# Eight edits to a state-space and two-expert kernel: spare rows, biases, register checks, a skewed addition and a spread tail

## The reference

```python
probs = softmax(layernorm(x) @ Wg)              # 8 experts
top_vals, top_idx = top_k(probs, 2)             # renormalised to sum 1: the shares
h = relu(layernorm(x) @ W1[e] + b1[e])          # 128 -> 256
y = h @ W2[e] + b2[e]                           # 256 -> 128
out = x + layernorm(share_a * y_a + share_b * y_b)
```

## Time and profile before

| | us |
|---|---|
| median of three runs | 990.61 |
| profiled execution | 989.48 |
| its span | 987.6 |
| PE busy | 836.5 (85%) |
| DVE busy | 769.7 (78%) |
| ACT busy | 659.0 (67%) |
| POOL busy | 521.9 (53%) |

### The profile page before, as it was taken

The page is one execution under the profiler, slowest core; times in us unless marked ns, Lnnn a source line. Parts: engine busy times, 40 slices in busy tenths (PEclk is TensorE's granted clock), DMA queues, the critical chain, the costliest instruction groups (busy, mean ns, idle before and its releaser), DMA issues.

```text
span 987.6 us, 26130 instructions
## 1 busy us (share of the span) xinstructions
PE 836.5 (85%) x8010; PEld 693.0 (70%) x8010; DVE 769.7 (78%) x2323; ACT 659.0 (67%) x1592; POOL 521.9 (53%) x1031
## 2 busy tenths in 40 slices
PE   4699999999999999999999999755787998989870
PEld 2487887777777777777777777544677888878770
DVE  5577879899998998989989899847667566656660
ACT  4578888777787787777877778533435556556650
POOL 4344544455454554646455555433456666666664
PEclk9799999999999999999999999986779999999995
DMA  7000000001010120210000000050624555555520
GB/s 204 8 2 4 5 2 15 7 29 44 8 54 15 55 77 9 86 23 10 10 12 8 12 7 9 19 144 18 171 64 123 153 137 141 141 141 142 146 87 0
DMA packets 59298, 57.82 MB, mean 59 GB/s; under 512 B 16727, under 2 KB 42861, under 8 KB 59163
## 3 DMA queue, kind: packets, MB, share of 16 engines
q1 hardware_dynamic: 54203, 47.61, 18.3%
q0 software_dynamic: 4960, 8.54, 2.5%
HBM read 44.52 MB, written 19.91 MB: 65 GB/s over the span
## 4 chain that ended last, share of the span: by engine, by line
DVE 30%; PE 21%; issue 20%; POOL 16%; SPq 6%; DMA 3%; ACT 2%; POOLq 1%; DVEq 0%; ACTq 0%
POOL out_dram L2249 8%; PE bank L875 4%; DVE xt L785 4%; DVE mg L1047 4%; POOL moe_y L2246 4%; DVE ob L1126 3%; PE bank L672 2%; SPq L1714 2%; DMA rows<-csplit 2%; DVE y L1059 2%; DVE state L1074 2%; PE bank L859 2%; DVE ob L1100 2%; PE bank L674 2%; PE bank L673 1%
## 5 line engine op out<-in xcount | busy, mean ns | idle before, releaser
L1038 POOL TENSOR_TENSOR y<-y,zt 128x256 f32<-128x256 f32 x64 | 46.7, 729 | 225.7 <-issue 136.4
L2249 POOL DMA_INDIRECT out_dram<-moe_y,moe_token x91 | 92.2, 1013 | 74.1 <-POOL moe_y L2246 69.4
L672 PE MATMUL bank<-thi,whi 128*128 128x512 f32 x224 | 105.7, 472 | 15.8 <-DVE cs L809 8.0
L2156 PE MATMUL bank<-moe_w,moe_hid 128*128 x728 | 117.3, 298 | 0.1
L959 ACT ACTIVATE m<-bank 128x512 f32<-128x512 f32 x128 | 69.3, 592 | 70.7 <-PE bank L861 70.5
L2117 PE MATMUL bank<-moe_h_turned,moe_w_now 128*128 128x128 f32 x728 | 103.8, 288 | 12.6 <-DMA moe_w_now<-pair_weights 12.5
L2117 PEld LDWEIGHTS bank<-moe_h_turned,moe_w_now 128*128 128x128 f32 x728 | 93.9, 202 | 16.4 <-issue 14.4
L2156 PEld LDWEIGHTS bank<-moe_w,moe_hid 128*128 128x128 f32 x728 | 98.2, 196 | 4.9 <-issue 0.4
L1047 DVE TENSOR_TENSOR mg<-bank,m 128x512 f32<-128x512 f32 x128 | 82.3, 685 | 17.5 <-PE bank L875 16.5
L674 PE MATMUL bank<-thi,wlo 128*128 128x512 f32 x224 | 89.7, 401 | 0.0
L673 PE MATMUL bank<-tlo,whi 128*128 128x512 f32 x224 | 89.6, 400 | 0.0
(11 more groups left out here) (268 smaller groups left out, 2361.0 us busy)
## 6 DMA issues: line engine op xcount, KB each, us to landing
moe_w_now<-pair_weights SPq DMA_DIRECT2D x91, 258.0 KB, 2.9
moe_block_in<-pair_rows SPq DMA_DIRECT2D x91, 66.0 KB, 1.9
pair_weights<-in_L_ffn_W_dram SPq DMA_DIRECT2D x31, 128.0 KB
parts<-csplit SPq DMA_DIRECT2D x128, 4.0 KB
rows<-csplit SPq DMA_DIRECT2D x128, 4.0 KB
pair_rows<-spare_row SPq DMA_DIRECT2D x29, 66.0 KB
out_dram<-moe_y,moe_token POOLq DMA_INDIRECT x91, 2.6
pair_rows<-xall,row_index POOLq DMA_INDIRECT x64, 2.6
```

The lines of the kernel that those rows point to most:

```text
L672: PE.matmul(bank[:], whi[:, w], thi[:], start=True, stop=False)
L2156: mm = PE.matmul(o, hid[:, u % HID, k, n, :], w2[:, bass.ds(e, 1), n, :].rearrange("p o d -> p (o d)"), start=False, stop=n == FB - 1, ski ...
L2249: PL.indirect_dma_start(rows_out, bass.IndirectOffsetOnAxis(token[:, u % IN:u % IN + 1], 0), y[:, u % YR, :], None, bounds_check=TOK - 1, ...
```

## The change

Eight edits. (1) The 29 writes of spare rows move from the end of the first half into `sp_pair_weights`, one group after its last part (n = NE + 1). (2) `b2` is no longer loaded as a broadcast, split and multiplied; it is stored beside `b1` in `pair_weights` (three bias columns for each expert), so that it comes with the unit's weights, and the product with `thirds` becomes a matmul in transpose mode of the broadcast bias column with the identity. `act_prepare` and `dve_prepare` are gone, and a weight slot is free again only when `pe_down` of unit u - 6 is done. (3) The register loads of SyncE and TensorE carry no runtime bounds check. (4) `pool_out` is cut in two: GpSimd adds unit u and then issues the DMA of unit u - 1 (`pool_return`). (5) The inputs of the shares are worked out before the scatter, three more operations in `pool_gap` for each group and one more column in each row; `pool_shares` becomes `pool_tokens`, which makes the row numbers alone, and `act_shares` reads the rows' columns. (6) IN is 24. (7) Units 0 to 19 have their relu on ScalarE, odd ones too. (8) The steps of the tail are spread further apart on every engine, and `pe_skip` and the second table move with them. The first residual stays on VectorE. Of the tail's steps the diff below shows TensorE's; on VectorE the top-two steps of the last two groups move from 3 and 4 to 4 and 5, and from 7 and 8 to 9 and 10, the last group's statistics from 5 to 6, and the row indices from 6 and 10 to 8 and 13 (the second table to 13 and 14). On GpSimd the last three groups' scatters move from 1, 6 and 10 to 3, 8 and 13. On ScalarE each logits step moves one to two later.

```diff
-ROW = D + 4
-WROW = 2 * FH + 2 * FB
-C_TOK, C_GAP, C_BIAS, C_SCALE = D, D + 1, D + 2, D + 3
+ROW = D + 5
+PCOLS = FB + 1
+WROW = 2 * FH + 2 * PCOLS
+C_TOK, C_BIAS, C_SCALE, C_UPPER, C_LOWER = D, D + 1, D + 2, D + 3, D + 4
...
+            sp.dma_start(b_rank[:, r, 0:FB], b1_d[NE - 1 - r].rearrange("(n p) -> p n", p=P), **small
+                         ).then_inc(b_loaded, 16)
+            sp.dma_start(b_rank[:, r, FB:PCOLS], b2_d[NE - 1 - r].rearrange("(n p) -> p n", p=P), **small
+                         ).then_inc(b_loaded, 16)
...
-        PL.tensor_tensor(xall[:, group(q), C_GAP], gap[:, 0, :], gap[:, 2, :], ALU.mult).then_inc(gap_step.sem, 1)
+        PL.tensor_tensor(gap[:, 3, :], gap[:, 0, :], gap[:, 2, :], ALU.mult).then_inc(gap_step.sem, 1)
+        pl.wait_ge(gap_step.sem, gap_step.of(q, 4))
+        pl.wait_ge(xscale.sem, xscale.of(q))
+        PL.tensor_tensor(gap[:, 1, :], gap[:, 3, :], xall[:, group(q), C_SCALE], ALU.mult).then_inc(gap_step.sem, 1)
+        pl.wait_ge(gap_step.sem, gap_step.of(q, 5))
+        PL.tensor_scalar(xall[:, group(q), C_UPPER], gap[:, 1, :], 0.0, None, ALU.min).then_inc(gap_step.sem, 1)
+        PL.tensor_scalar(xall[:, group(q), C_LOWER], gap[:, 1, :], -1.0, 0.0, ALU.mult, ALU.min
+                         ).then_inc(gap_step.sem, 1)
...
         if step == 1:
             pe_route_turn(pe, G_LAST - 1, fr)
-        if step == 2:
+        if step == 3:
             pe_route_logits(pe, G_LAST - 1, fr)
         if step == 5:
+            pe_route_turn(pe, G_LAST, fr)
+        if step == 7:
             pe_route_places(pe, G_LAST - 1, fr)
-            pe_route_turn(pe, G_LAST, fr)
-        if step == 6:
             pe_route_logits(pe, G_LAST, fr)
-        if step == 9:
+        if step == 12:
             pe_route_places(pe, G_LAST, fr)
...
+        if n == NE + 1:
+            sp.wait_ge(route_const.sem, ROUTE_CONSTS)
+            for k in range(NPAIR + 1):
+                sp.dma_start(rows_d[k * BUCKET:k * BUCKET + P], dummy[:]).then_inc(spare_rows, 16)
...
-    IN, YR, HN, HT, HID, WR, QR = 16, 12, 6, 3, 3, 6, 3
+    IN, YR, HN, HT, HID, WR, QR = 24, 12, 6, 3, 3, 6, 3
...
-            sp.wait_ge(up_done.sem, up_done.of(u - WR))
-            hidden_read(sp, u - WR)
+            sp.wait_ge(down_done.sem, down_done.of(u - WR))
...
-            PE.matmul(o, thirds[:], b2p[:, bass.ds(e, 1), :].rearrange("p o d -> p (o d)"), start=True, stop=False,
-                      skip_group_check=True)
+            PE.matmul(o, bias_of(u, k, FB).to_broadcast([P, P]), ident[:], start=True, stop=False, is_transpose=True,
+                      skip_group_check=True)
...
     def pool_out(pl, u):
         pl.wait_ge(normed.sem, normed.of(u))
         PL.tensor_tensor(y[:, u % YR, :], y[:, u % YR, :], block_in[:, u % IN, 0:D], ALU.add).then_inc(added.sem, 1)
+
+    def pool_return(pl, u):
         pl.wait_ge(added.sem, added.of(u))
         pl.wait_ge(token_kept.sem, token_kept.of(u // 4))
...
-            if u == 13:
+            if u == 17:
                 pe_skip(pe)
...
-                if u % 2 == 0:
+                if by_act(u):
                     act_hidden(act, u)
...
-            if u % 4 == 3 and u // 4 + 1 < QUADS:
-                pool_shares(pl, u // 4 + 1)
-            if u % 4 == 1 and u // 4 < QUADS:
+            if u % 4 == 2 and u // 4 < QUADS:
+                pool_tokens(pl, u // 4)
                 pool_share_sums(pl, u // 4)
-            if u >= NORM_LAG:
+            if NORM_LAG <= u < UNITS + NORM_LAG:
                 pool_out(pl, u - NORM_LAG)
+            if u > NORM_LAG:
+                pool_return(pl, u - NORM_LAG - 1)
```

More of the change, by code:

```diff
@@ L234, in attention @@
     mtop = keep("mtop", [P, 2, TILES])
-    gap = keep("gap", [P, 3, TG])
+    gap = keep("gap", [P, 4, TG])
     rows_of = keep("rows_of", [P, 2, NPAIR])
@@ L1139, in tail_uses @@
     def tail_uses():
[L1141 to L1144, removed]
+        a, b = GROUPS - 2, GROUPS - 1
+        return [(("places", GROUPS - 3), route, GROUPS - 3, PLACED), (("turn", a), x2t_ready, a, 1),
+                (("logits", a), lg_held, a, 1), (("turn", b), x2t_ready, b, 1), (("places", a), route, a, PLACED),
+                (("logits", b), lg_held, b, 1), (("places", b), route, b, PLACED)]
     for n, u in enumerate(tail_uses()):
@@ L1746, in sync_program @@
                 sp_pair_weights(sp, (b - 1) * GB + u)
-        sp.wait_ge(route_const.sem, ROUTE_CONSTS)
-        for n in range(NPAIR + 1):
-            sp.dma_start(rows_d[n * BUCKET:n * BUCKET + P], dummy[:]).then_inc(spare_rows, 16)
         sp.wait_ge(fr_done.sem, fr_done.of(G_LAST))
@@ L1891, in experts @@
     down_done = sig("down_done")
-    weight_in = sig("share_inputs", 3)
     weight = sig("shares_ready")
@@ L2097, in bias_of @@
     def bias_of(u, k, n):
-        return w1c[:, u % WR, 2 * FH + k * FB + n:2 * FH + k * FB + n + 1]
+        at = 2 * FH + k * PCOLS + n
+        return w1c[:, u % WR, at:at + 1]
     chosen, pair_now = {}, {}
+    BOUNDED = "the table is made from counts that the program bounds"
     def pe_choose(pe, u):
@@ L2182, in act_shares @@
     def act_shares(act, q):
-        act.wait_ge(weight_in.sem, weight_in.of(q))
-        w = wq[:, q % QR, 0:2, 0:len(in_quad(q))]
-        SE.activation(w, w, ACT.Exp).then_inc(weight.sem, 1)
+        for u in in_quad(q):
+            wait_loaded(act, u)
+        if q >= QR:
+            act.wait_ge(mixed.sem, mixed.of(last_of(q - QR)))
+            act.wait_ge(spread.sem, spread.of(q - QR))
+        a, many = in_quad(q)[0] % IN, len(in_quad(q))
+        SE.activation(wq[:, q % QR, 0:2, 0:many], block_in[:, a:a + many, C_UPPER:C_LOWER + 1].rearrange("p t k -> p k t"),
+                      ACT.Exp).then_inc(weight.sem, 1)
     def pool_share_sums(pl, q):
@@ L2320, in vector_program @@
                 dve_coef(dve, COEF_AT[u])
-            if u < UNITS and u % 2:
+            if u < UNITS and not by_act(u):
                 dve_hidden(dve, u)
@@ L2328, in gpsimd_program @@
     def gpsimd_program(pl):
[L2329 to L2330 removed]
+        for u in range(UNITS + NORM_LAG + 1):
             if u < UNITS:
                 att.pool_tail(pl, u)
[L2333 to L2335 removed]
+            if u % 4 == 2 and u // 4 < QUADS:
+                pool_tokens(pl, u // 4)
                 pool_share_sums(pl, u // 4)
[L2337 removed]
+            if NORM_LAG <= u < UNITS + NORM_LAG:
                 pool_out(pl, u - NORM_LAG)
+            if u > NORM_LAG:
+                pool_return(pl, u - NORM_LAG - 1)
     this = Part()
[L2341 to L2342 removed]
     this.dve_table = dve_table
```

140 lines of the change are left out of this document (52 added, 88 removed).

## The result

The changed kernel took 920.02 us, the median of four runs (917.29 to 923.56), beside 991.36 for the kernel before on the same chip: ratio 0.928, 95% interval 0.924 to 0.932. The prediction was 924.7 (907 to 942). The profiled execution took 917.29 us with a span of 915.6. Five more executions on another chip gave 918.58 to 922.01, median 919.86; a sixth there took 1144.48 us at a mean granted clock of 0.65 where the others had 0.96 to 0.97, stands in no comparison and has no trace, so that its cause, the clock rival's or another, is open.

A forecast was written before the change was run, and what follows sets the result against it. GpSimd was taken to bound units 20 to 90. Of the 65 us to be saved, 29 come before unit 20, 29 from the pace and 7 from the tail: span 922.8, time 924.7 us, range 907 to 942.

The forecast's parts named there:

- the clock rival: Late units: granted clock falls to half, each unit costs 4.44 us, 151 us more, 1076 us in all; chance 0.02.
- The skew and GpSimd: Late units: DMA behind the next unit's addition idles 0.51 us less, GpSimd needs 2.0 us a unit and leaves the bound.
- the first rival: The skew saves nothing: GpSimd stays the bound in late units at 2.51 us a unit, 944 us in all; chance 0.08.
- TensorE's pace: Late units: TensorE bounds next at 2.28 us a unit (2.15 to 2.5), including about 0.11 for the bias transposes.
- The 0.06 for late arrivals: Late units: 0.06 us a unit added to TensorE's 2.22 for late arrivals, giving 2.28.
- SyncE: Second half's loads: 1.08 us a load without checks, under 1.7 with the pick, so no bound.
- Until unit 0: Before unit 0: the stall goes, 16.0 us less, and six loads save 2.9; unit 0 at 674.6.
- Units 0 to 19: Early units: 2.2 us a unit, 2.4 with routing; the last scatter and loads put unit 20 at 736.
- GpSimd's debt: Between the last two scatters: five additions and returns, 8.9 us, plus 1.4 of token and norm work, delaying the last scatter.
- The tail: After unit 90 starts: 17.1 us to GpSimd's last issue, then 10.1 to the end of the span.
- A pace of 2.5: Late units: TensorE, DMA or a latency holds at 2.5 us a unit, 15 us more, 940 us; chance 0.09.
- Less lost early: Before unit 20: GpSimd's debt is small, unit 20 at 725, 914 us in all; chance 0.08.

The follow-up runs named there:

- The experiment with the relus: Changed kernel with the relus of the odd ones of units 0 to 19 back on VectorE: 915.23 us, ratio 0.922.
- its own experiment: Changed kernel with each unit's output DMA issued right behind its own addition, as before the change: 954.26 us, ratio 0.965.

## Why the prediction was right

*The skew and GpSimd* were right in kind and in size: 0.57 us less a unit where 0.51 was taken (0.80 to 0.23), the bound left GpSimd, and without the skew it would have kept it at 2.47, as the first rival had it. The Trainium skill ("GPSIMD Engine Reference", 2.1 Instruction dispatch) says that an instruction's completion gates what waits on its semaphore and not the next instruction of the engine. The rows of the output DMA agree: 0.79 us where the DMA waits for the addition just before it, 0.17 to 0.37 where it does not.

*TensorE's pace* was right in mechanism and too dear by 0.17 us: 2.28 predicted, 2.11 measured, 12 us over 70 units. The term that was mis-sized is the bias. The step of the transpose (0.11) was read rightly, but the bf16 product was priced by its own step alone; the 0.05 that it puts on the fp32 products behind it stand in the trace of before too and were not looked for:

```profile
750.87 0.66 PE L2156 MATMUL bank<-moe_w,moe_hid 128*128 x4
751.37 0.22 PE L2153 MATMUL bank<-moe_b_parts,moe_thirds 128*128 x1
```

that is 0.50 us for the four instructions, against 0.45 behind a transpose. The 0.06 for late arrivals was nothing with the unchecked load (and 0.06 exactly with the checked one). The factor of four in the Trainium skill ("TensorE: Matmul & The Clock Gate", Terms) gave the right 2.11 by a wrong reason: two transposes cost 0.22 us a unit here, 0.11 each, half of a plain fp32 product.

*SyncE* was no bound, as said, and the six loads lost 2.7 us (8.18 to 5.48) for 2.9. But "it is no bound" rested on the edit more than the text had it: with the checks its loop takes 2.17 us a unit and the kernel 2.25.

*Until unit 0*: 674.6 predicted, 674.3 measured. The stall went, and taking out the split of `b2` was enough for it; that the early spare writes were needed too, as the text has it, is refuted, though they may have been enough for the 9.6 us of waiting. The text also calls all engines stopped for 15.7 us; TensorE stood for 14.3, and ScalarE and VectorE worked on the split in the last 5.9.

*Units 0 to 19* is the step that failed: 61.4 us predicted, 67.1 measured, and the pace within it by more. "The turns 2.2 a unit, TensorE the same; with routing 2.4" was 3.33 up to unit 12 (674.31 to 714.25). ScalarE was counted by its busy time, and what TensorE waits for is ScalarE's order: the h of a pair stands behind the relus of the unit just multiplied. In the changed kernel,

```profile
706.00 0.33 PE L2051 MATMUL bank<-ident,moe_h 128*128 128x128 f32 x1 [0.44 <-ACT moe_h L2041]
...
714.09 0.33 PE L2051 MATMUL bank<-ident,moe_h 128*128 128x128 f32 x1 [3.46 <-ACT moe_h L2041]
```

the second transpose of nearly every pair waits for `act_h`, 0.44 us at the least and up to 3.5, in all 15.8 us from 672 to 745. The experiment with the relus shows 5 us of it; the two longest of these waits, 3.0 and 3.5 us, follow stands of ScalarE that are not explained (below), and how much of the 5.7 us is theirs is open. GpSimd's debt between its last two scatters was 9.7 us (710.14 to 719.81) for 10.3, but it hid nothing and cost nothing, since VectorE's last index (L1344) came only at 719.47. The last scatter was issued at 726.40 for 721.7, and unit 20 came at 741.45 for 736. These 5.7 us too many and the 11.9 too few of the pace partly cancel: they are 6.2 of the 7.4 us by which 924.7 lies above the profiled execution, 917.29. That the sum came within 5 us of the median is in part luck, since two errors of opposite sign met.

*The tail*: 16.4 us from unit 90 to the last issue for 17.1, 10.05 from there for 10.1.

*The rivals.* No gain of the skew: refuted by its own experiment. A pace of 2.5: no; weights landed in time at a DMA share of 0.68. Less lost early: no. The clock: it was 1.00 from 770 to 875 us in every profile taken, with transposes as three of nineteen steps of a unit. The Trainium skill ("TensorE: Matmul & The Clock Gate", Part 4: PE-mode transpose) says that transpose mode does not count as PE-busy in the same way; that had no visible effect there. Only the one execution at 0.65, without a trace, keeps this rival from being closed.

*What each part was worth*, by what its undoing cost: the skew 34 us; the checks on SyncE 11 to 14 and on TensorE 6 to 7; the early spare rows 3 at most; the spread of the tail nothing that can be told; the relus on ScalarE 4.6 the other way. Three parts were not undone: the new way of `b2`, with which the stall of 16 us went but which shares that with the spare rows; the share operations, a part of GpSimd's room; and IN = 24. The gains do not add up from the kernel before, where the skew alone brought 25: each bound only shows when the one above it is gone.

## What to carry to other kernels

On GpSimd, an indirect DMA that waits for the operation just before it starts 0.6 us later than one that does not; here 34 us in all were to be had by putting one independent instruction between. The price is the DMA's: short operations that wait for the one just before them pay far less, as `pool_gap` of the changed kernel shows,

```profile
702.84 0.20 POOL L1354 TENSOR_TENSOR gap<-rank_of 128x4 f32<-128x4 f32 x1
703.13 0.19 POOL L1357 TENSOR_SCALAR gap<-gap 128x4 f32<-128x4 f32 x1
703.40 0.20 POOL L1359 TENSOR_TENSOR gap<-gap 128x4 f32<-128x4 f32 x1
```

where each starts 0.27 to 0.29 us behind the one it waits for, with under 0.1 us of idle between. When such a bound is lifted, work out the next one on each engine with the edit and without it: SyncE's loop with its checks (2.17 us) and TensorE's (2.11) were a few hundredths apart. Moving work off an engine because it looks full is worth nothing unless that engine is the one that is waited for: VectorE had the time for the relus, and ScalarE's order did not.

## What the runs showed of the hardware

Two fp32 products take 0.50 us behind a bf16 product and 0.45 behind an fp32 one (a transpose or a plain product); with the bias's operands, in the kernel before, as with zeros.

ScalarE stood still for about 3 us ahead of the relus of unit 11, though TensorE's records show its products done at 709.2. In its first profile the changed kernel has

```profile
712.51 1.14 ACT L2117 ACTIVATE moe_hid<-bank,moe_w_now 128x128 f32<-128x128 f32 x4 [2.97 <-remote]
```

("remote": released by something the profile does not name.) Of the ten profiles whose ScalarE has the same order up to there, nine have this stand, 2.8 to 3.2 us long, at the same instruction; the tenth, with the checks on TensorE, has 2.3 us one unit earlier and 0.9 here. With three shorter ones (the longest 2.38 us at 685.26 and 1.71 at 729.70) it is 8 us of units 0 to 19 in the first profile. The kernel with the relus on VectorE, whose ScalarE has other instructions there, has two others, of 3.8 and 1.0 us. What stopped it was not found and not tried.

The first half, the same code in each, differs by up to 7.8 us between profiles by where TensorE's clock is low; that is more than some of these edits bring, and the reason to compare medians of several executions, not single profiles.
